# Second attention of a four-layer kernel: TensorE's order within a step, weighted values moved behind the scores

## The reference, cut to what matters

```python
def _L1_xattn_ref(q, k, v, w_q, w_k, w_v, w_o):      # 8 x 256 x 256
    H, D_K, D_V = 16, 64, 64
    qh = (q @ w_q.T).reshape(b, n, H, D_K).transpose(0, 2, 1, 3)
    kh = (k @ w_k.T).reshape(b, n, H, D_K).transpose(0, 2, 1, 3)
    vh = (v @ w_v.T).reshape(b, n, H, D_V).transpose(0, 2, 1, 3)
    scores = jnp.einsum('bhid,bhjd->bhij', qh, kh) / math.sqrt(D_K)
    scores = jnp.where(causal[None, None], scores, -jnp.inf)
    attn = jax.nn.softmax(scores, axis=-1)
    out = jnp.einsum('bhij,bhjd->bhid', attn, vh)
    out = out.transpose(0, 2, 1, 3).reshape(b, n, H * D_V)
    return out @ w_o.T

x = x + _L0_ffn_ref(...)                                   # top-1 of 8 experts
x = x + _L1_xattn_ref(_layernorm(x), ctx_1024, ctx_1024, ...)
x = x + _L1_ffn_ref(_layernorm(x), ...)                    # top-2 of 8 experts
```

## Time and profile before

| | |
|---|---|
| median of 3 runs | 1735.67 (1729.64 to 1739.29) |
| the profiled execution's own time | 1732.06 |
| its span in the profile | 1730.2 |
| TensorE's granted clock, mean of the span | 0.932 |
| TensorE busy with matmuls | 1479.9, 86% of the span |
| DVE, ACT, POOL busy | 832.5, 522.7, 417.6 |
| the second attention | about 515 to 940 |

### The profile page before, as it was taken

One profiled execution on the slowest core, in us unless ns is written; L12 is line 12 of the kernel. 1 busy time (PEld: TensorE's weight loads), 2 busy tenths in 40 slices (PEclk: granted clock), 3 DMA queues, 4 the chain that ended last, 5 costly groups with the idle time before them and its releaser, 6 DMA issues. The chain is left out here.

```text
span 1730.2 us, 31832 instructions
## 1 busy us (share of the span) xinstructions
PE 1479.9 (86%) x11282; PEld 1285.6 (74%) x11282; DVE 832.5 (48%) x2319; ACT 522.7 (30%) x1300; POOL 417.6 (24%) x651
## 2 busy tenths in 40 slices
PE   4789986599958999999994599999999978985775
PEld 3466664489957888888884599999999967864664
DVE  4677663322215666666665311111111127876996
ACT  1233332112214445445441111111111112334553
POOL 2011101133223444433322100000000036730222
PEclk7799999699989999999997699999999989996888
DMA  7655420783410000000000444224426232100000
GB/s 149 109 92 107 76 38 20 271 272 107 132 40 20 7 13 14 20 19 14 7 8 13 162 170 170 97 97 170 170 95 244 85 98 68 50 6 1 13 13 25
DMA packets 99469, 141.90 MB, mean 82 GB/s; under 512 B 10209, under 2 KB 83425, under 8 KB 99233
## 3 DMA queue, kind: packets, MB, share of 16 engines
q1 hardware_dynamic: 81968, 111.92, 22.3%
q0 software_dynamic: 6368, 18.62, 3.7%
q10 hardware_dynamic: 11024, 9.97, 1.9%
HBM read 113.22 MB, written 14.42 MB: 74 GB/s over the span
## 5 line engine op out<-in xcount | busy, mean ns | idle before, releaser
L1603 PEld LDWEIGHTS f_ph<-f_xgT,f_w 128*128 128x128 f32 x3232 | 374.0, 194 | 10.5 <-issue 4.2
L1603 PE MATMUL f_ph<-f_xgT,f_w 128*128 128x128 f32 x3232 | 375.3, 277 | 5.3 <-DMA f_w<-in_f_w 2.7
L1613 PE MATMUL f_py<-f_w,f_hT 128*128 128x256 f32 x992 | 224.7, 379 | 0.2 <-ACT f_hT L1645 0.2
L1613 PEld LDWEIGHTS f_py<-f_w,f_hT 128*128 128x128 f32 x992 | 183.6, 190 | 23.3 <-issue 0.8
L1677 DVE TENSOR_TENSOR f_hT<-f_ph,f_gate_o 128x512 f32<-128x512 f32 x78 | 53.9, 691 | 262.9 <-ACT f_gate_o L1639 262.9
L1576 POOL DMA_INDIRECT f_xg<-normed_x,order x62 | 59.5, 960 | 498.8 <-PE f_px L1592 464.2
L987 ACT ACTIVATE a_work<-a_ps,a_bias 128x128 f32<-128x128 f32 (+1 forms) x256 | 104.1, 419 | 172.5 <-issue 98.0
L1187 POOL TENSOR_TENSOR a_work<-a_work,a_recip 128x256 f32<-128x256 f32 (+1 forms) x128 | 103.2, 828 | 147.8 <-DVE a_recip L1106 146.7
L1639 ACT ACTIVATE f_gate_o<-f_ph 128x512 f32<-128x512 f32 x78 | 46.6, 597 | 295.2 <-PE f_ph L1603 295.1
L574 DVE CUSTOM_DVE_ANT_0 a_shut_s<-a_ps,a_neg 128x256 f32<-128x256 f32 x256 | 93.0, 419 | 39.5 <-PE a_ps L253 39.0
L486 ACT ACTIVATE a_pT<-a_ps 128x1024 f32<-128x1024 f32 x64 | 65.5, 1024 | 118.8 <-PE a_ps L253 118.8
(11 more groups left out here) (319 smaller groups left out, 2881.0 us busy)
## 6 DMA issues: line engine op xcount, KB each, us to landing
f_w<-in_f_w SPq DMA_DIRECT2D x70, 1024.0 KB, 7.8
sorted_y<-f_yg ACTq DMA_DIRECT2D x62, 128.0 KB, 1.7
a_qs<-a_part SPq DMA_DIRECT2D x48, 128.0 KB, 4.4
a_ks<-a_part SPq DMA_DIRECT2D x42, 128.0 KB, 6.2
normed_x<-a_xn SPq DMA_DIRECT2D x16, 256.0 KB, 2.1
x<-in_x SPq DMA_DIRECT2D x8, 256.0 KB, 6.6
a_mask<-in_mask SPq DMA_DIRECT2D x8, 256.0 KB, 6.4
a_maskT<-in_maskT SPq DMA_DIRECT2D x8, 256.0 KB, 6.5
```

The costliest lines, as they stand in the source:

```text
L1603: mm = pe.matmul(ph[:, q, n, f * P:(f + 1) * P], w[:, s, k, (q * FQ + f) * P:(q * FQ + f + 1) * P], xgT[:, s, k, :], start=(k == 0), stop= ...
L1613: mm = pe.matmul(py[:, s, 0:D], hT[:, s, f, :], w2[:, s, f, :], start=(f == 0), stop=(f == FT - 1))
```

## The change

The calls of a TensorE step are reordered; no call is added or removed, and no other engine's list changes. `values` moves from behind `output` to right behind `scores`, so ahead of the value projection, the row transposes, the routing product, and `output`. `project` and `output` change places at the step's end.

```diff
                 if is_unit(n - SCORE):
                     scores(n - SCORE)
+                if is_unit(n - VALUE):
+                    values(n - VALUE)
                 if is_unit(n) and n % 4 == 1:
                     project_values(n)
                 if in_front(n, 3) is not None:
@@
                     turn_rows(behind(n, BEHIND), n, xn3, norm3, turned3)
+                if is_unit(n):
+                    project(n)
                 if is_unit(n - OUT):
                     output(n - OUT)
-                if is_unit(n - VALUE):
-                    values(n - VALUE)
-                if is_unit(n):
-                    project(n)
```

## The result

The changed kernel takes 1763.54 us (median of 6 runs, 1755.81 to 1769.35), the kernel before beside it 1736.09 (6 runs, 1729.64 to 1739.61). The ratio is 1.0168, with a 95% interval from 1.0149 to 1.0186: slower. The forecast was 1744 with a range up to 1757, so the time lies 6.5 us outside the range. The profiled execution took 1760.78, 28.7 more than that of before; its span is 1758.9 against 1730.2. The mean granted clock over the whole span is 0.920, where it was 0.932.

A forecast was written before the change was run, and what follows sets the result against it. TensorE was taken to set the pace (matmuls 48.88 of 50 us); late DVE copies add 1.85 per full batch: +7.4 for four, +0.75, +0.95, -0.3, -0.7, sum +8.1, giving 1744 us, range 1731 to 1757.

The forecast's parts named there:

- the mechanism: Second attention: values loses its cover and starts 0.07 behind DVE's copy of the transposes when that ends late.
- the walk: Eight intervals between starts of values' loads, one batch of the second attention: 51.9 us against 50.07 today.
- V1 to V2: Start of values' loads in step 1 modulo 8 to the next step's: 7.65 by TensorE, 7.70 taken.
- upper end: Rival where the loop stretches: all intervals at their highest, 52.7 per batch, 1751 us; chance 0.15.
- The tail: End of the stage: output fills part of the wait for the last values, -0.7 us.
- one switch less: TensorE changes between full and half array three times per step instead of four, gaining 0.20 per step.
- The rival that made 11 us of it: Nothing waits, so 0.20 comes back in each of 56 steps: 11 us gained, time 1725; chance 0.10.
- The clock falls: Rival: idle TensorE drops to 1.2 GHz in step 1 modulo 8, +5.7 in each of 6 batches: 1778; chance 0.03.
- at an unchanged clock: Expected sign in the profile after: matmul busy below 48 of 50 us with the granted clock unchanged.
- project ahead of output: At the step's end project comes 0.7 earlier and the residual later, priced 0 to 0.2 in one step of eight.
- without TensorE: Loop of DVE's copy, ACT's exponentials and parts said to close once per step without TensorE, 5.28 in early steps.
- D's intervals: Times between ends of DVE's copy of the transposes, taken from the trace of before, such as 5.27 and 5.77.

The follow-up runs named there:

- e1: Changed kernel plus 14 products with unused results on TensorE between scores and values in steps with n % 8 of 1 and 3: 1747.1 us, ratio 1.0066.
- e4: Changed kernel with DVE's batch work ahead of parts instead of behind it from step 8 on: 1723.6 us, ratio 0.9927.
- e6: Kernel before, TensorE's order untouched, with DVE's batch work ahead of parts from step 8 on: 1719.58 us, ratio 0.9928.
- e2: Changed kernel with output again ahead of project, values staying behind scores: 1771.22 us, ratio 1.0198.
- e7: Changed kernel plus the 14 unused products only in steps with n % 8 of 1: 1753.49 us, ratio 1.0125.
- e8: e4 plus three DVE fills of a spare buffer behind the batch work in steps with n % 8 of 0 and 2: 1767.69 us, ratio 1.0193.
- e3: Changed kernel with values moved behind value projection, row transposes and routing, still ahead of project and output: 1726.48 us, ratio 0.9937.

## Why the prediction was wrong

**Right: the mechanism and its terms.** `values` lost its cover and follows DVE's copy at 0.07; the stalls are where I put them, 2.27 in kind 1 and 2.00 in kind 3 ("about 2.2" and "2.0"); every interval of the walk is within 0.17 in e1. The largest miss of these is V1 to V2, 7.87 against 7.70: the "7.85" of the upper end, which I had in the text. Without the filler's 2.2 us e1's periods sum to 358.0, 10.9 above before; the forecast had 7.4 + 0.75 + 0.95 - 0.3 = 8.8, and most of the difference is in the first two batches (1.6 each for 0.75 and 0.95). The tail gave 1.1 for 0.7. One sign differs: I expected the idle time to be put down to DVE or ACT, and the waits name only issue; DVE's copy stands behind it all the same, 0.06 to 0.07 ahead of V each time.

**Right, and small: one switch less.** Where the copy isn't late the step falls from 5.08 to 4.93 (kind 4, n = 44), so the switch gives 0.15, not 0.20; e4's kinds 4 and 6 give 0.18 and 0.19 against e6. The Trainium skill, "TensorEngine Tiling (Array Packing)", Key Properties, says that a changed mode drains TensorE; these runs agree with the sign. The rival that made 11 us of it fell: with DVE's work early, e4 against e6 shows the whole order worth nothing that can be told (48.38 and 48.42 per batch, ratios 0.9927 and 0.9928).

**Wrong: "The clock falls ... Nothing in the earlier trace rows speaks for it. 0.03", and with it "at an unchanged clock".** This is the step that failed: the sum holds two stalls of 2 us per batch and no term for what the clock does behind them. The earlier trace rows is a stretch in which TensorE never stood still for 2 us, so it had no say on what such a wait does. After the change the clock fell to 1.2 GHz behind three of the five stalls of kind 1 with output products (and behind the one of n = 9), and behind all five stalls of 2.00 in kind 3 (n = 19 to 51). The cost is the changed kernel's sum, 376.4, less e1's without its filler, 358.0: 18.4 us of the 29.3. e1, which differs from the changed kernel in what TensorE does while it waits, shows it.

**The trace of before did speak for it, in a stage that the change doesn't touch.** In the first attention TensorE stands still for 2.29 or 2.30 us three times. Two of these waits in the trace of before, then the 3 us of work behind each (columns as above):

```profile
156.41 0.46 PEld L358 LDWEIGHTS a_ps<-ident,a_xn 128*128 128x128 f32 x4 [2.30 <-issue]
...
186.69 0.72 PEld L358 LDWEIGHTS a_ps<-ident,a_xn 128*128 128x128 f32 x4 [2.29 <-issue]
```

```profile
156.40:159.40 3.00, 2.96 (x33) 1.81 (x34) 1.80 (x6) 0.63 (x2) 0.00 (x0) 1.00 1.14 131
186.70:189.60 2.90, 2.88 (x21) 1.31 (x21) 1.52 (x5) 0.60 (x1) 0.00 (x0) 0.51 1.14 134
```

Behind one the clock is 1.00, behind the other 0.51, and the same four loads take 0.46 and 0.72. In the eleven traces of this document there are 33 such waits, of 2.28 to 2.30; over the 2.5 us behind them the clock is 1.00 in 16, 0.50 in 16 and 0.65 in one. A stall of the length that I forecast had thus been seen to halve the clock, and 0.03 was too low a chance for it.

**The size of that rival was off too.** I priced it as 5.7 us more in each of 6 batches, 34 in all and 1778, all of it in kind 1. In kind 1 the fall costs 1.56: the value projection doubles almost (4.17 instead of 2.59 us of loads) and project behind it is at full speed again. In kind 3 it costs 1.5 to 3.0, and up to 0.8 more in the step behind. In the stretches looked at the clock was back at 1.00 behind some 4 to 7 us of work, so a fall had a bounded price. The forecast's 1743.8, with 18.4 for the clock, 2.1 for the longer walk (10.9 for 8.8) and 0.4 less for the tail, gives 1763.9; the median is 1763.54.

**Half seen: project ahead of output.** I counted only its cost for the residual. e2 shows that the earlier project speeds up the `parts` loop; without it the kernel is at 1771. So the loop doesn't close "without TensorE", as I had written: ACT's `parts` in it waits for project. The gain was already inside my walk, since I took D's intervals from rows with project last and found them to hold (5.27 and 5.76), but I didn't name it.

**Not seen: what lateness costs the kernel before.** I said that TensorE stood still only 1 us in 50 and took the rest of the pace as given. e6 shows 1.6 per batch to be had by moving DVE's batch work alone.

What stays open is why the same stall (2.27 and 2.28, in n = 33 and 41) once leaves the clock alone and once halves it. The waits in the first attention, about half of them with a fall, show that this is no property of the new order. e7 shows only that the falls in kind 3 don't need those in kind 1. That the half clock comes from the idle time and not from some other property of the order is shown by e1 (idle time filled, order the same), e4 (idle time short, order the same) and e8 (idle time brought back).

## What to carry to other kernels

When an edit lets TensorE stand still for 2 us in a stage where it never did before, price the clock behind the stall as well as the stall: here it was 18 of the 29 us lost. Before moving a block to right behind its producer, ask which engine's copy it waits for and what was covering that copy; a block that covers costs nothing, and the cheap mend is often on the other engine's list, as with DVE's batch work ahead of `parts` (-0.7%, with either order on TensorE). A quiet stretch of the profile is no evidence of how the chip behaves in a regime that it doesn't contain; look for a stretch of another stage that does contain it, as the first attention here.

## What the runs showed of the hardware that I had not expected

- Idle times of 2.0 to 2.65 us on TensorE in the second attention, behind stretches at a granted clock of 1.00, were followed by 0.50 in most cases: behind the stall of n = 35 for some 7 us (0.59 from 743.20 to 747.00, 0.50 up to 750.50), behind that of n = 41 for about 4 us of work. The ones of 0.66 and less in e4 and e3 were followed by 1.00, as were 1.09 and 1.35 in the changed kernel and 1.74 in e8 (n = 59). The length alone doesn't decide it: 1.93 (n = 5) was followed by 0.55 in e2 and e7 and by 1.00 in the changed kernel, and 3.06 (n = 9 of e8) by 1.00.
- Products whose results nobody uses paid for themselves: 14 more of them in two steps of eight made the kernel 16 us faster (1747.1 against 1763.54), with a clock of 1.00 where it had been 0.93.
- Two stalls of equal length, with equal work ahead, differed in what followed. The runs of the changed kernel lie 13.5 us apart (1755.81 to 1769.35), those of before 10.0.
